# Key roots moved from VectorE and ScalarE to GpSimd, both query projections behind the keys, the atoms' product inside batch 0

## What is computed

```python
def _rms(x, scale):
    var = jnp.mean(x * x, axis=-1, keepdims=True)
    return x * jax.lax.rsqrt(var + EPS) * (1.0 + scale)
q = _rms(einsum('btd,od->bto', x, Wq)...); k = _rms(...); v = einsum(...)
q, k = _rope(q, pos), _rope(k, pos)
k_blocks = k_blocks.at[blk, :, off, :].set(k)      # v too; then gathered by block table
p = softmax(where(allowed, q @ k_all * SCALE, -inf)); o = p @ v_all; out0 = o @ Wo.T
# mixture of layer 0: top 2 of 8 experts per token
deltas = softmax(expert_atom_weights, -1) @ atoms   # [8, 4096]
weighted = deltas * sigmoid(importance)             # added into W at mask_idx
```

## Time and profile before

| | |
|---|---|
| median of 3 runs | 1119.12 us (1115.15 to 1119.79) |
| profiled execution | 1120.77 us |
| its span | 1119.0 us |
| mean granted clock of TensorE | 0.932 of full |
| busy: TensorE, VectorE, ScalarE, GpSimd | 944.0, 556.6, 418.8, 329.0 us |

### The profile page before, as it was taken

The page is one execution under the profiler, slowest core; times in us unless marked ns, Lnnn a source line. Parts: engine busy times, 40 slices in busy tenths (PEclk is TensorE's granted clock), DMA queues, the critical chain, the costliest instruction groups (busy, mean ns, idle before and its releaser), DMA issues.

```text
span 1119.0 us, 18432 instructions
## 1 busy us (share of the span) xinstructions
PE 944.0 (84%) x4690; PEld 609.2 (54%) x4691; DVE 556.6 (50%) x2242; ACT 418.8 (37%) x1283; POOL 329.0 (29%) x368
## 2 busy tenths in 40 slices
PE   6995799888986798706989996999199999999994
PEld 2463475454543454403434444888077777777772
DVE  4678757675753878563333442455333333333331
ACT  3452645554543555301111111222144444555440
POOL 3003215646553152111333441133212212212221
PEclk9986989999999899967999998999689999999998
DMA  8947314244234243357777774794643333333330
GB/s 283 301 189 256 106 39 127 66 115 118 69 87 133 78 137 132 114 167 213 205 209 158 136 125 132 283 395 170 195 113 63 67 67 69 69 67 68 61 58 1
DMA packets 76552, 152.12 MB, mean 136 GB/s; under 512 B 15719, under 2 KB 24599, under 8 KB 74832
## 3 DMA queue, kind: packets, MB, share of 16 engines
q1 hardware_dynamic: 38624, 84.87, 23.0%
q0 software_dynamic: 25520, 45.11, 19.7%
q10 hardware_dynamic: 12352, 21.51, 5.8%
HBM read 94.05 MB, written 69.00 MB: 146 GB/s over the span
## 4 chain that ended last, share of the span: by engine, by line
PE 62%; DVE 11%; DMA 10%; issue 9%; ACT 3%; DVEq 2%; SPq 1%; another core or an unknown queue 1%; POOL 0%; ACTq 0%; POOLq 0%
PE ps L657 50%; DMA acc<-R,tok_i 5%; PE ps L663 4%; PE ps L723 3%; DVE R L1516 2%; DVE R L1534 2%; PE ps L711 2%; DVE R L1505 1%; ACT R L1011 1%; DMA R<-acc 1%; DMA R<-rows 1%; PE ps L704 1%; DMA rows<-zrow 1%; DMA R<-m_buf 1%; PE ps L743 1%
## 5 line engine op out<-in xcount | busy, mean ns | idle before, releaser
L657 PE MATMUL ps<-R 128*128 128x128 f32 (+4 forms) x2768 | 689.3, 405 | 38.5 <-issue 19.6
L657 PEld LDWEIGHTS ps<-R 128*128 128x128 f32 x2768 | 421.2, 195 | 266.4 <-issue 251.2
L629 POOL DMA_INDIRECT out_x<-R,tok_i x39 | 60.5, 1551 | 252.5 <-DVEq L1859 156.9
L663 PE MATMUL ps<-ident,R 128*128 128x128 f32 x440 | 67.5, 286 | 75.0 <-DMA R<-rows 59.7
L663 PEld LDWEIGHTS ps<-ident,R 128*128 128x128 f32 x440 | 53.7, 147 | 108.9 <-issue 94.0
L1022 ACT ACTIVATE R<-R,nmx 128x384 f32<-128x384 f32 x128 | 78.3, 621 | 84.1 <-DVE nmx L1505 71.5
L558 POOL DMA_INDIRECT rows<-R,slot_i x64 | 65.0, 1015 | 141.0 <-DVEq L1608 62.9
L629 POOL DMA_INDIRECT acc<-R,tok_i x39 | 60.9, 1561 | 134.4 <-DVE R L1768 131.3
L1505 DVE CUSTOM_DVE_ANT_0 R<-ps,R,q_scale 128x384 f32<-128x384 f32 x128 | 73.6, 612 | 41.1 <-issue 41.1
L711 PE MATMUL ps<-ident,R 128*128 128x128 f32 x384 | 57.2, 285 | 34.3 <-DVE R L1516 22.6
L1181 ACT ACT_TABLE_LOAD x18 | 23.1, 1283 | 147.8 <-PE ps L657 147.8
(11 more groups left out here) (292 smaller groups left out, 901.0 us busy)
## 6 DMA issues: line engine op xcount, KB each, us to landing
R<-rows SPq DMA_DIRECT2D x78, 258.0 KB, 3.1
R<-in_fc ACTq DMA_DIRECT2D x16, 1024.0 KB, 5.6
m_buf<-R SPq DMA_DIRECT2D x8, 1024.0 KB
R<-m_buf SPq DMA_DIRECT2D x16, 512.0 KB
R<-acc SPq DMA_DIRECT2D x32, 256.0 KB
R<-in_x_t SPq DMA_DIRECT2D x4, 1024.0 KB, 10.9
R<-in_x_t SPq DMA_DIRECT2D x8, 512.0 KB, 3.6
new_kv<-R SPq DMA_DIRECT2D x16, 256.0 KB, 2.0
```

What stands on the lines that cost most here:

```text
L629: po.indirect_dma_start(out=sums[s], out_offset=bass.IndirectOffsetOnAxis(ap=tok_i[:, s:s + 1], axis=0), in_=y_sb[s], in_offset=None, boun ...
L657: m = pe.matmul(out, lhs(k), rhs(k), start=(k == 0 and first), stop=(k == KC - 1 and last))
L663: m = pe.transpose(out[:, k * P:(k + 1) * P], src[:, k * P:(k + 1) * P], ident[:])
```

## The change

- **Roots of the keys.** `sums_k` and ScalarE's `roots` go. GpSimd's new `key_roots(n)` waits for the squares of pair n (`kv_sq`), computes the inverse roots of its two tiles by the 14 instructions of `scales` (now shared as `inverse_roots`), and signals `rst`. Pairs 0 and 1 stand ahead of the five loads L505 to L509, pairs 2 to 7 behind them, with the two gathers of old rows behind pair 5. `ss` and `rstd` get four slots instead of two, `sq` four buffers, so ScalarE takes the squares of the next pair ahead of scaling the present one.
- **Queries.** TensorE projects query tile 1 right behind tile 0 into bank 2 (`o_p1`), ahead of the small products; ScalarE and VectorE read it there. The two key turns go to banks 3 and 4 (`o_k`, `o_kc`).
- **Product of atoms.** It leaves the opening and stands in batch 0, half behind the scores of step 0, half behind those of step 1, now in bank 1 (`cell_deltas`). VectorE's `cell_weights` follows its maxima of step 1; TensorE waits for it ahead of the first `mix`. GpSimd's gathers for batch 1 still wait for the product (`delta`).
- **VectorE's order.** Index work comes earlier (up to `idx_n` of the first batches behind pair 4), the query tables behind pair 5, half of the sparse comparison behind pair 6, the other half behind the masks of batch 0.
- **Waits.** The wait for the output weights (`att_w`) moves from batch 0 to batch 1. SP waits for `o_p1` instead of bank 0's use before it loads the next queries. `imp` and `mark_w` change places in SBUF.

```diff
+            def inverse_roots(src, out, k):
+                x, y, t = nw_x[:, 0:k], nw_y[:, 0:k], nw_t[:, 0:k]
+                po.tensor_scalar(x, src, 1.0 / HD, RMS_EPS, ALU.mult, ALU.add)
+                po.drain()
+                po.tensor_scalar(y.bitcast(I32), x.bitcast(I32), -0.5, 1597463007.0, ALU.mult, ALU.add)
+                po.drain()
+                for n in range(3):
+                    po.tensor_tensor(t, y, y, ALU.mult)
+                    po.drain()
+                    po.tensor_tensor(t, t, x, ALU.mult)
+                    po.drain()
+                    po.tensor_scalar(t, t, -0.5, 1.5, ALU.mult, ALU.add)
+                    po.drain()
+                    po.tensor_tensor(out if n == 2 else y, y, t, ALU.mult)
+                    if n < 2:
+                        po.drain()
+            def key_roots(n):
+                po.wait_ge(S["kv_sq"], 2 * n + 2)
+                wait(po, S["kv_nr"], 2 * n - 2)
+                inverse_roots(ss[:, r].rearrange(flat), rstd[:, r].rearrange(flat), 2 * NG)
+                po.drain().then_inc(S["rst"], 2)
+            for n in range(2):
+                key_roots(n)
             po.wait_ge(S["w_kv"], 16)
...
-            po.wait_ge(S["idx_ok"], 1)
-            old_rows(0)
+            for n in range(2, NT // 2):
+                key_roots(n)
+                if n == 5:
+                    po.wait_ge(S["idx_ok"], 1)
+                    old_rows(0)
...
+            def cell_deltas(x):
+                if x == 0:
+                    pe.wait_ge(S["pre_c"], 1)
+                    pe.wait_ge(S["atoms_d"], 32)
+                for t in range(ST // 2 * x, ST // 2 * (x + 1)):
+                    for y in range(2):
+                        m = pe.matmul(ps[64 * y:64 * y + 64, 1, t * NE:(t + 1) * NE], at_v[64 * y:64 * y + 64, t, :],
+                                      eaw_t[64 * y:64 * y + 64, :], start=True, stop=True)
+                m.then_inc(S["delta"], 1)
...
                     dots(B, j, s)
+                    if j < 2 and first:
+                        cell_deltas(j)
...
             project_q(opening, 0)
+            pe.wait_ge(S["kv_nr"], NT - 5)
+            queries(1, 2).then_inc(S["o_p1"], 1)
             pe.wait_ge(S["raw_dma"], 16 * 5)
...
-            project_q(opening, 1)
-            pe.wait_ge(S["pre_c"], 1)
-            pe.wait_ge(S["atoms_d"], 32)
+            turn_q(opening, 0)
             pe.wait_ge(S["kv_nr"], NT)
-            for t in range(ST): ...
-            turn_q(opening, 0)
             pe.wait_ge(S2["kvd"][0], 64)
             for p in range(2):
-                turn_k(opening, p, 0)
-            pe.wait_ge(S["wgt_ok"], 1)
-            pe.wait_ge(S["att_w"], 16 * (2 * KC + 1))
+                turn_k4(ps[:, 3 + p, :], 0, p).then_inc(S["o_k"], 1)
...
+            for t in range(2):
+                squares(t)
+            for n in range(NT // 2):
+                for t in (2 * n + 2, 2 * n + 3):
+                    if t < NT:
+                        squares(t)
+                for t in (2 * n, 2 * n + 1):
+                    scaled(t)
...
+            for n in range(NT // 2):
                 for x in range(2):
                     rope_k(2 * n + x)
+                if n in (0, 1, 2, 3, 4):
+                    next(index)
+                if n in (2, 4):
+                    next(index)
+                if n == 5:
+                    tables(0, tabq_a, tabq_b)
+                if n == 6:
+                    sparse_eq(0, 4)
```

More of the change, by code:

```diff
@@ L117, in program @@
         nrm = [words(R2, 14336 + KD * s, [KD]) for s in range(2)]
-        sq = [words(R2, 14848 + KD * s, [KD]) for s in range(2)]
+        sq = [words(R2, base, [KD]) for base in (14848, 15104, 5120, 5376)]
         sin_t = words(R2, 15360, [NT, HD // 2])
@@ L206, in program @@
         tot = sb("tot", [P, ST, NE])
-        ss = sb("ss", [P, 2, NG])
-        rstd = sb("rstd", [P, 2, NG])
-        root = sb("root", [P, 2, NG])
+        ss = sb("ss", [P, 4, NG])
+        rstd = sb("rstd", [P, 4, NG])
         ssq = sb("ssq", [P, 16])
@@ L219, in program @@
         junk_a = sb("junk_a", [P, 4])
+        mark_w = junk_a[:, 2:4]
         lg = sb("lg", [P, 2, NE])
@@ L530, in scales @@
                 po.wait_ge(S["q_ss"], 2 * b + 2)
-                po.tensor_scalar(nw_x[:], ssq[:], 1.0 / HD, RMS_EPS, ALU.mult, ALU.add)
+                inverse_roots(ssq[:], nw_y[:], 16)
                 po.drain()
[L533 to L543, removed]
                 po.tensor_scalar(q_scale[:, b % 2, :], nw_y[:], -SCALE, None, ALU.mult)
@@ L719, in mix @@
                     wait(pe, S["s_ot"], 2 * B + qt)
+                if B == 0 and m == 0:
+                    pe.wait_ge(S["wgt_ok"], 1)
                 for c in range(3):
@@ L735, in project @@
                 half(x, 0).then_inc(bk, 1)
+            at_v = atoms.rearrange("a (p t) -> a t p", t=ST)
+            def cell_deltas(x):
[7 more added lines that the diff above has]
+                m.then_inc(S["delta"], 1)
             def cell_sums(at):
@@ L756, in period @@
                 for j in range(NH):
-                    if j == 0:
-                        wait(pe, bc, uses(B - 1)["k1"] + 1)
+                    if j == 0 and first:
+                        pe.wait_ge(bc, uses(-1)["q0"] + 1)
+                        pe.wait_ge(S["o_kc"], 2)
+                        pe.wait_ge(S["q_rp"], 2)
+                    elif j == 0:
+                        pe.wait_ge(bc, uses(B - 1)["k1"] + 1)
+                        if B == 1:
+                            pe.wait_ge(S["att_w"], 16 * (2 * KC + 1))
                     if j == NH // 2:
@@ L1072, in _ @@
             squares_q(opening, 0)
+            ac.wait_ge(S["o_p1"], 1)
+            squares_of(1, 2)
             ac.wait_ge(S["pre_w"], 1)
@@ L1077, in _ @@
             ac.activation(lora_b[:, D:DG], ps[:, 1, 128:128 + NE], ACT.Copy).then_inc(S["pre_c"], 1)
-            squares_q(opening, 1)
             q_out(opening, 0, 0)
             for p in range(2):
-                k_out(opening, p, 0)
+                ac.wait_ge(S["o_k"], p + 1)
+                copy_bank(3 + p, k_t[0][:, p, :]).then_inc(S["o_kc"], 1)
             periods(ac, period)
@@ L1414, in rope_q @@
                 ve.wait_ge(S["q_ss"], t + 1)
-                rope(ps[:, 0, :], rq_a, rq_b, tabq_a, tabq_b, NH, t).then_inc(S["bc"], 1)
+                last = rope(ps[:, 2 if t == 1 else 0, :], rq_a, rq_b, tabq_a, tabq_b, NH, t)
+                if t != 1:
+                    last.then_inc(S["bc"], 1)
                 ve.drain()
@@ L1432, in _ @@
             next(index)
-            sums_k(0, 0, BOTH)
-            for n in range(NT // 2 - 1):
-                if n < 6:
-                    next(index)
-                if n == 6:
-                    tables(0, tabq_a, tabq_b)
-                if n + 1 < NT // 2 - 1:
-                    sums_k(n + 1, 2 * n + 2, BOTH)
-                else:
-                    sums_k(n + 1, NT - 2, (0,))
+            for n in range(NT // 2):
                 for x in range(2):
                     rope_k(2 * n + x)
-            sums_k(NT // 2, NT - 2, (1,))
-            for x in range(2):
-                rope_k(NT - 2 + x)
-            next(index)
+                if n in (0, 1, 2, 3, 4):
[6 more added lines that the diff above has]
+                    sparse_eq(0, 4)
             def cell_weights():
@@ L1669, in period @@
                         build_mask(1)
+                    if j == 1 and first:
+                        cell_weights()
                     if j == 2 and not last:
@@ L1714, in _ @@
             rope_q(0)
-            sparse_eq(0, 8)
             rope_q(1)
```

79 lines of the change are left out of this document (23 added, 56 removed).

## The result

| | before | after |
|---|---|---|
| median of 4 runs each | 1118.73 us (1115.15 to 1119.79) | 1129.51 us (1127.43 to 1131.1) |
| profiled execution, its span | 1120.77, 1119.0 us | 1129.13, 1127.1 us |
| mean granted clock | 0.932 | 0.919 |

The ratio is 1.0108, with a 95% interval of 1.0085 to 1.0131: slower by 9.5 to 14.7 us. The forecast was 1117, in a range of 1106 to 1126.

A forecast was written before the change was run, and what follows sets the result against it. It took the opening, with TensorE waiting and a lagging key pass, as the bound. Savings of 0.3 (K), 1.0 (G), 0.3 (to first weights) and 1.0 (batch 0) gave 1118.2 profiled, median 1116.5, written 1117; range 1106 to 1126.

The forecast's parts named there:

- the first of the four about a disturbed key pass: GpSimd's key roots: drains behind DMA issues add 0.3 + 3.0 us for pairs 2 and 6, bounds 0.3 and 5.3.
- K: End of the last key tile on ScalarE: forecast 89.0 us against 89.3 before.
- The store of tile 0: Key pass: store expected at 51.5 us, between 49.5 and 54, so pair 4's roots run only from 54.6.
- The 0.7 a pair: Key pass: GpSimd's roots lose 0.7 us of a possible 1.4 a pair to VectorE's rotations sharing the SBUF ports.
- The 2.3 for the comparison: Last key pair: the sparse comparison beside its roots adds 2.3 us, 3.4 if locked through.
- G: Start of the first gather: about K + 4.2, following the store since index work ends by 68; 1.0 us saved.
- First weights: First weights turned on TensorE: G + 24.1 against G + 24.4 before, gathers landing at G + 10; 0.3 us saved.
- The roots of the queries: GpSimd in batch 0: query roots come at G + 16, at the end of the first scores, so in time.
- The product: Atoms' product in batch 0: two halves of 3.6 us behind score steps 0 and 1, moved and not hidden.
- Rival 2: Key pass: VectorE locks GpSimd out, K from 97 on, up to 10.5 us on K; 1127 us, chance 0.17.
- Rival 3: Atoms' product in batch 0 runs at half its rate, 7.2 us more; 1124 us, chance 0.06.
- Rival 1: Key pass: roots run free, drains cost nothing, K 77.7, 13.9 us saved in all; 1105 us, chance 0.33.

The follow-up runs named there:

- e9: Changed kernel with GpSimd's key-root instructions ordered by its own semaphore instead of drains, loads and gathers in place; 0.9931 of before.
- e7: e2 with one 1 MB load of output weights left on GpSimd ahead of pair 2, four on ScalarE; 1.0054 of before.
- e8: e6 with the mask load behind the store of tile 6, the atoms' product ahead of batch 0, SP's output weights and zeros held; 0.9900 of before.
- e5: e2 with GpSimd's two gathers of old rows moved from behind pair 5 to behind pair 7; 0.9960 of before.
- e11: e6 with semaphores instead of drains in the roots of the keys and of the first queries; 0.9864 of before.
- e4: Changed kernel with key roots back on VectorE and ScalarE, and loads, index work and sparse comparison in their old places; 0.9985 of before.
- e6: e5 with the first half of the sparse comparison back behind the masks of batch 0; 0.9907 of before.
- e10: e8 with semaphores instead of drains in the roots of the keys and of batch 0's queries; 0.9882 of before.
- e12: e10 with two pieces of index work moved from batch 0 to behind pairs 5 and 6 of the key pass; 0.9872 of before.
- e2: Changed kernel with the five loads issued from ScalarE's queue behind the squares of tiles 0 and 1; 0.9952 of before.
- e1: Changed kernel with the five loads issued from ScalarE's queue behind the scaling of pair 1, at about the same time; 0.9955 of before.
- e3: Changed kernel with the 2 MB mask load behind the store of tile 6, the five loads still on GpSimd; 1.0029 of before.

## Why the prediction was wrong

**The step that failed** is the first of the four about a disturbed key pass: "I take 0.3 + 3.0 for pairs 2 and 6, which stand behind issues; bounds 0.3 and 5.3." For pair 6 the drain was 2.61 as taken. For pair 2 it was 15.24, three times the upper bound. I read two rows, 5.3 and 2.98, as a price of issuing. What stood in front of them was small: four gathers of 0.56 MB together, and a scatter of less than 0.01 MB. And the 5.3 wasn't all drain. GpSimd's timeline in the kernel before, ahead of the two instructions:

```profile
103.56 0.63 POOL L531 TENSOR_SCALAR nw_x<-ssq 128x16 f32<-128x16 f32 x1 [3.20 <-ACT R L1011]
...
187.69 1.55 POOL L566 DMA_INDIRECT m_buf<-tot,cell_i  x1 [2.56 <-DMA m_buf<-tot,cell_i]
```

Of the 5.3, 3.20 were a wait for ScalarE's squares of the queries, and GpSimd stood at the drain for 1.48. What ends the drain was in the earlier trace rows: q0's last packets in the us from 104, the drain's end at 105.67. Five loads of 2.3 MB beside a 2 MB mask take until 55 to move, and the drain took as long. That it was the drain is shown by e9, that it goes by the transfer by e7.

**K.** Forecast 89.0, measured 99.5. Pair 2 ended at 60.1 instead of 44.5, 15.6 late: 12.2 from the drain, 1.5 from pair 1, the rest from a gap of 2.1 ahead of the loads. The store of tile 0, which I had let hold pair 4 from 50.3 to 54.6, had long landed and gave 4.3 back. Pairs 3, 4 and 5 took 5.6, 5.9 and 5.4 against my 5.8, 6.6 and 6.3, and gave 1.8 back.

**The lock.** The 0.7 a pair was about right: pair 0, undisturbed, took 4.74, and pairs 1, 3, 4 and 5, beside rotations and index work, 6.1, 5.6, 5.9 and 5.4. The 2.3 for the comparison was right too (7.8 for pair 7, against 5.8 + 2.3). GpSimd mostly gets in between two VectorE instructions that follow each other at once: beside the four comparisons of the changed kernel it did one step for each (0.92, 0.78, 0.75, 0.78). But not always. The 2.67 of e8 above began beside one of eight comparisons that follow each other at once, each 0.93 behind the last, and ended at 98.41, with the whole group (98.38). In the first 140 us of all these runs it is the only root step above 1.0; why it was held and the others weren't, no run shows.

The rule of the Trainium skill, page "SBUF — State Buffer", section "SBUF: two separate sides", that the lock is held for the whole instruction, agrees with the trace for single instructions (steps of 0.80 beside comparisons of 0.96 in e5, 0.20 undisturbed). In the changed kernel GpSimd was not shut out of a whole group.

**G and after.** G = K + 4.6 (forecast 4.2), released by the stores and no more by the index work, as said. First weights at G + 24.9 (24.1): the keys landed at G + 10.9 instead of 10. In the other runs in which TensorE waited for it that figure went from 8.4 (e11) to 12.05 (e4), and I had no term for it. The roots of the queries were ready at G + 16.0, as said, though from the 5.3 that mixed two waits. The product took 3.69 + 3.69 at half clock, as said (3.6 + 3.6). Up to the maxima of the fourth step batch 0 saved 0.7 (1.0 forecast): 9.14 behind the first weights instead of 9.85.

**The rivals.** Rival 2 had nearly the right number, 1127 of 1129.5, for the wrong cause. Both of its signs came (K behind 97, last roots behind 94, at 97.2), but no pair was shut out. It had 2.0 for a longer drain in its price and not 12; that its sum came close is luck. Rival 3 is out. Rival 1 is what the idea is worth once loads, gathers and comparison are off the roots: its K of 77.7 is e6's. e6's first weights are 12.0 earlier than before and its ratio is 0.9907; rival 1's 1105, a ratio of 0.987, was reached only with the drains gone too (e10 to e12).

## What to carry to other kernels

In all these runs a drain on GpSimd behind a DMA that GpSimd issued was a wait for that DMA. Put chains of dependent small instructions ahead of its DMAs, give its plain loads to another queue, at a time at which the issues don't hold that engine (e2, not e1), or order the chain by a semaphore of its own instead of drains, which is also cheaper (0.285 a step instead of 0.35). And when a price is read from a row, ask what ended it, and take off what was another wait: here the time of the queue's last packet stood beside it, and 3.20 of the 5.3 belonged to ScalarE.

## What was not expected of the hardware

- The length of a GpSimd drain by what stands in front: 2.61 us behind two gathers, 5.72 behind four, 10.84 behind one load of 1 MB, 15.24 behind five loads of 2.3 MB, 12.20 behind the same with the mask out of the way; each ends within 2 us of the last packets of its queue. Where a load stood last it ended 0.2 to 0.3 behind that load's landing (55.4 and 55.74 in the changed kernel, 52.75 and 53.06 in e3, 48.38 and 48.56 in e7). Behind the four gathers it ended 0.17 to 0.18 behind the start of TensorE's key turns, which waited for the same gathers, in the changed kernel, e1, e2, e3 and e7 (115.05 and 115.22 in the changed one). So it goes by the landing.
- An issue on ScalarE's queue took 0.4 to 0.65 us, and 6.29 and 3.62 for the fourth and fifth of five in a row (e1; 0.92 and 1.37 in e2, 14 to 19 us earlier): there the issuing engine pays. What fills up, no run shows.
- In e9 GpSimd's first load starts 7.02 us behind the last root instruction of pair 1, a gap without a cause in the profile (2.12 in the changed kernel). It stays open; the one thing that the traces show there is a packet of an instruction queue (q14), in the us from 37 in e9 and from 33 in the changed kernel. Without the gap K would have been nearer to e6's.
